# Moving the small vectors of a graph-transformer kernel behind its large buffers in SBUF

## The reference

```python
q, k, v = heads(x @ wq + bq), heads(x @ wk + bk), heads(x @ wv + bv)
scores = einsum('bhqd,bhkd->bhqk', q, k) * 48 ** -0.5 + adj[:, None]
ctx = einsum('bhij,bhjd->bhid', softmax(scores), v)
x1 = rmsnorm(x + merge(ctx) @ wo + bo, alpha1, gamma1)
ff = silu(x1 @ w1 + b1) @ w2 + b2
out = layernorm(x + rmsnorm(x1 + ff, alpha2, gamma2))
```

## The kernel before, in words

| buffers | start modulo 512 before | after |
|---|---|---|
| wq_s, wk_s, wv_s, wo_s, w1_s, w2_s, stage | 128 | 128 |
| rows, ident | 256 | 128 |
| x_in, x_res, x_last, bias, xT, qk_flat, qk, v_first, v_rest, probs | 288 | 128 |
| ctxT, x1, x1T, h_raw, h, y, squares | 480 | 128 |

## Time and profile before

### The profile page before, as it was taken

The page is one execution under the profiler, slowest core; times in us unless marked ns, Lnnn a source line. Parts: engine busy times, 40 slices in busy tenths (PEclk is TensorE's granted clock), DMA queues, the critical chain, the costliest instruction groups (busy, mean ns, idle before and its releaser), DMA issues.

```text
span 2966.6 us, 62752 instructions
## 1 busy us (share of the span) xinstructions
PE 2923.2 (99%) x25216; PEld 2871.9 (97%) x25216; DVE 1974.3 (67%) x3621; ACT 1441.6 (49%) x4260; POOL 697.8 (24%) x968
## 2 busy tenths in 40 slices
PE   7999999999999999999999999999999999999998
PEld 6999999999999999999999999999999999999998
DVE  5766666666666676666666666666666667666665
ACT  5455455454554454544545545545445445454442
POOL 0222222222222222222222222222222222222222
PEclk9999999999999999999999999999999999999999
DMA  5211211211212112112122121121121211211200
GB/s 163 74 57 47 69 53 50 69 47 56 68 35 69 56 47 69 52 52 69 41 63 59 45 68 54 50 69 48 55 69 36 68 56 47 69 52 51 63 28 28
DMA packets 155491, 171.93 MB, mean 58 GB/s; under 512 B 18624, under 2 KB 155200, under 8 KB 155200
## 3 DMA queue, kind: packets, MB, share of 16 engines
q1 hardware_dynamic: 155200, 167.91, 19.1%
HBM read 92.35 MB, written 25.17 MB: 40 GB/s over the span
## 4 chain that ended last, share of the span: by engine, by line
PE 96%; DVE 1%; ACT 1%; SPq 1%; issue 0%; POOL 0%; DMA 0%; POOLq 0%; ACTq 0%; DVEq 0%
PE ps_work L450 48%; PE ps_rows L518 27%; PE ps_rows L450 6%; PE ps_att L462 4%; PE ps_att L471 4%; PE ps_att L482 2%; PE ps_att L486 2%; PE ps_work L560 2%; PE ps_rows L560 1%; SPq L331 0%; ACT probs L704 0%; DVE w_s L864 0%; SPq L383 0%; ACT squares L719 0%; DVE neg_max L876 0%
## 5 line engine op out<-in xcount | busy, mean ns | idle before, releaser
L450 PE MATMUL ps_work<-x1T,w_s 128*128 128x256 f32 x6912 | 847.7, 283 | 2.9 <-ACT h_raw L760 2.2
L450 PEld LDWEIGHTS ps_work<-x1T,w_s 128*128 128x128 f32 x6912 | 835.6, 188 | 3.5 <-ACT h_raw L760 2.4
L518 PE MATMUL ps_rows<-w_s,h 128*128 128x384 f32 x4608 | 822.2, 339 | 10.7 <-DVE x1T L922 7.0
L518 PEld LDWEIGHTS ps_rows<-w_s,h 128*128 128x128 f32 x4608 | 801.4, 189 | 18.7 <-issue 7.4
L760 ACT ACTIVATE h_raw<-ps_work,b_col 128x256 f32<-128x256 f32 x768 | 322.7, 471 | 478.5 <-PE ps_work L450 471.3
L704 ACT ACTIVATE probs<-probs,neg_max 128x128 f32<-128x128 f32 x1024 | 396.0, 388 | 238.5 <-DVE neg_max L876 238.5
L946 DVE TENSOR_TENSOR h<-h_raw,h 128x512 fp32r<-128x512 f32 x384 | 359.3, 936 | 13.2
L944 DVE CAST h<-h_raw 128x512 fp32r<-128x512 f32 x384 | 165.7, 431 | 302.7 <-ACT h_raw L760 302.2
L419 POOL TENSOR_TENSOR x_last<-x_last,rows 128x768 f32<-128x768 f32 x64 | 117.7, 1839 | 773.8 <-PE ps_att L462 773.8
L407 POOL TENSOR_SCALAR mean_sq<-sum_sq 128x1 f32<-128x1 f32 x256 | 69.0, 270 | 975.4 <-ACT squares L719 975.3
L450 PE MATMUL ps_work<-wv_s,xT 128*128 128x384 f32 x1152 | 235.2, 348 | 2.1 <-ACT qk_flat L740 1.2
(11 more groups left out here) (86 smaller groups left out, 3440.7 us busy)
## 6 DMA issues: line engine op xcount, KB each, us to landing
qk<-qk_flat SPq DMA_DIRECT2D x384, 96.0 KB, 2.4
x_in<-in_x SPq DMA_DIRECT2D x64, 384.0 KB, 3.2
x_res<-in_x SPq DMA_DIRECT2D x64, 384.0 KB, 3.9
x_last<-in_x SPq DMA_DIRECT2D x64, 384.0 KB, 3.2
out<-y SPq DMA_DIRECT2D x63, 384.0 KB, 2.5
bias<-in_adj SPq DMA_DIRECT2D x64, 128.0 KB, 3.8
qk<-qk_flat SPq DMA_DIRECT2D x128, 64.0 KB, 2.1
qk<-qk_flat SPq DMA_DIRECT2D x128, 32.0 KB, 2.0
```

Of the source, the lines that this page charges most:

```text
L450: mm = pe.matmul(ps_out, stationary(sta), moving(mov), start=(i == 0), stop=(i == n - 1))
L518: mm = pe.matmul(ps_rows[b][:, 0:d], h[:, sta, m, b * P:(b + 1) * P], w2_s[:, mov, m, :], start=(m == 0 and i == 0), stop=(m == fc - 1 and ...
```

## The change

Seven small vectors (the three bias columns, the constant -0.5, and the three softmax statistics) are allocated behind `squares` instead of between the large buffers. No instruction is added, removed or moved; only addresses change. The whole diff:

```diff
         stage = sb("stage", [P, STAGE_SLOTS, d])
 
-        bq_col = sb("bq_col", [P, kd])
-        bk_col = sb("bk_col", [P, kd])
-        b1_col = sb("b1_col", [P, fc])
         rows = sb("rows", [P, 7, d])
         BO, BV, B2, ALPHA1, GAMMA1, ALPHA2, GAMMA2 = range(7)
         ident = sb("ident", [P, P])
-        neg_half = sb("neg_half", [P, 1])
 
         x_in = sb("x_in", [P, PAIR, d])
...
         probs = sb("probs", [P, PAIR, HEADS, P])
-        neg_max = sb("neg_max", [P, PAIR, HEADS])
-        row_sum = sb("row_sum", [P, PAIR, HEADS])
-        row_inv = sb("row_inv", [P, PAIR, HEADS])
         ctxT = sb("ctxT", [P, PAIR, 2, kd, P], F32R)
...
         squares = sb("squares", [P, d])
+        bq_col = sb("bq_col", [P, kd])
+        bk_col = sb("bk_col", [P, kd])
+        b1_col = sb("b1_col", [P, fc])
+        neg_half = sb("neg_half", [P, 1])
+        neg_max = sb("neg_max", [P, PAIR, HEADS])
+        row_sum = sb("row_sum", [P, PAIR, HEADS])
+        row_inv = sb("row_inv", [P, PAIR, HEADS])
         sum_sq1 = sb("sum_sq1", [P, PAIR])
```

## The result

The changed kernel is slower: 2975.86 us (2975.1 to 2978.68, 9 runs) against 2967.73 us (2966.7 to 2968.9, 9 runs). The ratio is 1.0029, with a 95% interval of 1.0019 to 1.0039, so 8.1 us more. The forecast was 2923 us.

A forecast was written before the change was run, and what follows sets the result against it. TensorE's matmul pitches were taken to bound the kernel. The middle between the modest end (-22.3 us) and the line (-66.8 us), -44.5 us, took the profiled 2968.35 to 2923.9, median 2923 us; range 2878 to 3000 us.

The forecast's parts named there:

- What bounds the kernel: Whole kernel: TensorE busy 99% of the span, so time is the sum of some 25,000 matmul pitches.
- The starts sort the pitches: Five fp32r products: moving start minus stationary start, modulo 512, sorts pitches; distance 352 costs more than 160.
- the line: All fp32r products: cost grows with distance, carried on from 352 and 160 to 0: 115.2 and 170.2 ns, together -66.8 us.
- The modest end: All fp32r products come to the better pitch their width shows now: up -18.0, v -4.3, together -22.3 us.
- Up: Up product, 6912 matmuls of 256 columns: 4.8 ns less each by the line, -33.2 us.
- Q and k: Q and k products, 3456 matmuls of 256 columns: 2.2 ns less each by the line, -7.6 us.
- Down and output: Down (4608 matmuls) and output product (1152), 384 columns: 3.1 and 3.4 ns less each, -14.3 and -3.9 us.
- V: V product, 1152 matmuls of 384 columns: 6.8 ns less each by the line, -7.8 us.
- Rival 2: Fp32r products: equal starts make moving stream and weight load meet, slower by 29.9 us (2997.5) or 82.6 (3050); chance 0.30.
- Rival 3: Fp32r products: greater gain, bounded by the scores product's 112.1 ns at distance 0, -132 us, 2836 us; chance 0.07.
- The rule of the two read ports: TensorE operand reads: ports independent, so starts could not matter and the sum would be 0, 2967.6 us.
- V's 177.0 ns: V product's pitch before the change, 384 columns at distance 352: (1.40 - 0.338) / 6.

The follow-up runs named there:

- The streams: Kernel without the layer: streams of 54 fp32r matmuls, moving buffer at 16 distances from the stationary one; steady means from 113.3 ns (256 columns) and 173.3 ns (384).

## Why the prediction was wrong

**What bounds the kernel** was right. Only the pitch moved; PE stayed at 99%, its waits are the same, VectorE and the DMAs cost nothing.

**The starts sort the pitches** was right in the main. Up, q and k, which now share one distance, share one pitch, and shifting all buffers changes nothing. The modulus is 256 where the prediction took 512. But the distance alone does not fix the pitch: with only xT put back, q and k came to 118.8 ns and not to 117.4, and down at 160 has 173.3 or 176.7 ns.

**The step that failed** is the size that was put on distance 0, "the cost grows with the distance ... Carried on by 160 bytes to distance 0, that takes off 2.2 and 3.1 ns more". Two points at each width were taken for a line. The streams show no line: at 256 columns, 32 has 116.7 ns and 96 has 120.0, 112 has 113.3 and 128 has 118.7. Distance 0 has 120.0 ns where the line gave 115.2, the same as 352 by another pattern, and 173.3 ns at 384 columns where the line gave 170.2. The modest end failed too: it had all products at the better pitch of their width.

- Up: forecast -33.2 us; it already had 120.0 ns on average and keeps it. Measured -0.8 us.
- Q and k: forecast -7.6 us; they lost the better of the two pitches. Measured +8.1 us.
- Down and output: forecast -14.3 and -3.9 us; 173.3 ns is what they had, and no stream of 384 columns had a lower steady mean. Measured +1.4 us for down's irregular start; the output product kept its time within 3 ns a slot.
- V: forecast -6.8 ns a matmul; its nine have 168, 177, 185, 176, 182 and 173 ns between starts in place of 174 to 180, and the sum has not changed.

**Rival 2** had the right sign, and its term for q and k (+9.0 us) is close to what happened (+8.1). Its terms for down and output (+17.0 and +3.9) did not come. Its mechanism, two streams that meet, was not shown; that a narrower stationary operand changes the pitches says only that the weight load takes part.

**Rival 3's** bound from the scores, 112.1 ns, is close to the best steady pitch found (113.3 at distance 112), but it does not belong to distance 0.

**The rule of the two read ports.** The Trainium skill, "SBUF — State Buffer", section "Who interferes with whom", has TensorE wait on no one, and its two read ports independent. As to the other engines the runs agree: in the streams, where none of them computes, the pitches at 0, 96 and 160 are those of the kernel. But by that rule the starts would not matter, and they are worth 2.0% here, from 2927 to 2986 us. The gap of N/2.4 + 2.5 ns that the Trainium skill gives for an isolated matmul, in "TensorE: Matmul & The Clock Gate", section "Back-to-back issue gap", was reached by no fp32r stream: the best had 6.7 ns over the column time at 256 columns and 13.3 at 384. The prediction set its 109.2 ns for 256 columns beside the 109 ns of the transposes, but these move 128 columns of plain float32, so the two numbers do not bear on each other.

**A small misreading.** V's 177.0 ns was worked out with a duration of 338 ns, which its rows do not show (they have a mean of 348, over the whole run). From the single starts v had 176.3 ns before. With that the line through the two distances gives 5 us less gain.

## What to carry to other kernels

Where TensorE streams fp32r products with a weight load for each matmul, look at the distance between moving and stationary operand modulo 256 bytes. Here it decided which pitches were possible, and equal starts were nothing special. Measure it with streams at 16 distances in one short kernel, put each product at a good one, and time the kernel itself: a stream is a first guess only, for distance 104 had 130.0 ns there and 120.1 in the kernel. Here 16 bytes ahead of one buffer gave 34 us and a second buffer 6 us more. Then look at the products that were not touched, because one product's pattern depends on what ran ahead, and a move that is neutral by itself (x1T to distance 0) cost 18 us elsewhere.

## What was not expected of the hardware

- The pitch is periodic in the distance with 256 bytes (but for two of the distances, which took another pattern) and sensitive to steps of 8 bytes: in the streams 130.0 ns at 104, 113.3 ns at 112, for 256 columns at the 2.4 GHz level.
- A product at one distance has several steady patterns: down 173.3 or 176.7 ns at distance 160, q and k 117.4 or 118.8 at 160. Which one it takes repeats in every steady slot of a trace, and it was seen to depend on a product two places ahead.
- The least pitch of fp32r matmuls was 272 cycles for 256 columns and 416 for 384. Fewer stationary columns did not lower it, though they lowered the mean over the distances at 256 columns, from 118.3 to 115.7 ns. What the 16 and 32 cycles are spent on stays open.
